# Reordering the last table search, the products of tile 0 and tile 1, and one gather wait in an embedding tower

## The reference

```python
e = jnp.stack([tbl_0[ids[:, 0]], ..., tbl_26[ids[:, 26]]], axis=1)   # 512 x 27 x 128
dot_products = jnp.einsum('bnd,bmd->bnm', e, e)
r, c = np.tril_indices(27, k=-1)
h = jnp.concatenate([dot_products[:, c, r], dense_ctx], axis=1)      # 512 x 367
h = jnp.maximum(h @ W_top1 + b_top1, 0.0)                            # 512
h = jnp.maximum(h @ W_top2 + b_top2, 0.0)                            # 256
y = h @ W_top3
```

## Time and profile before

| what | value |
|---|---|
| median of 3 runs | 108.38 us (107.68 to 108.66) |
| the profiled execution's own time | 108.2 us |
| its span, first to last instruction | 106.3 us |
| TensorE busy, share of the span | 91% |
| VectorE, ScalarE, GpSimd busy | 64% each |
| granted TensorE clock | 1.00 throughout |

### The profile page before, as it was taken

The page is one execution under the profiler, slowest core; times in us unless marked ns, Lnnn a source line. Parts: engine busy times, 40 slices in busy tenths (PEclk is TensorE's granted clock), DMA queues, the critical chain, the costliest instruction groups (busy, mean ns, idle before and its releaser), DMA issues.

```text
span 106.3 us, 3471 instructions
## 1 busy us (share of the span) xinstructions
PE 97.1 (91%) x1496; PEld 78.6 (74%) x1496; DVE 68.5 (64%) x97; ACT 67.6 (64%) x112; POOL 67.7 (64%) x71
## 2 busy tenths in 40 slices
PE   6999879989999998999999989959949999989992
PEld 6646567857788675878788878649849898878981
DVE  5699999999999999999999714016012612007101
ACT  4486999998999969999876008125304555344241
POOL 3777887887778778877877777777777772000000
PEclk9999999999999999999999999999999999999999
DMA  2899749678688773948112222222212211000000
GB/s 49 244 257 199 217 88 294 188 197 240 150 228 272 194 217 70 266 101 227 51 49 56 54 57 52 72 57 56 54 51 56 56 49 49 6 0 6 6 0 1
DMA packets 5305, 12.06 MB, mean 113 GB/s; under 512 B 1765, under 2 KB 2277, under 8 KB 5290
## 3 DMA queue, kind: packets, MB, share of 16 engines
q1 hardware_dynamic: 3282, 7.75, 26.0%
q0 software_dynamic: 1984, 4.07, 15.1%
q10 hardware_dynamic: 24, 0.02, 0.1%
HBM read 11.83 MB, written 0.00 MB: 111 GB/s over the span
## 4 chain that ended last, share of the span: by engine, by line
PE 55%; DVE 34%; issue 7%; ACT 2%; POOL 0%; DVEq 0%; ACTq 0%; POOLq 0%
DVE marks L644 23%; PE gram_ps L537 12%; PE ring L510 11%; DVE low L621 9%; PE ring L590 5%; PE ids_ps L572 4%; PE gram_ps L510 4%; PE ring L521 3%; PE ids_ps L565 3%; PE ring L470 2%; PE ring L600 2%; PE ring L572 2%; PE ids_ps L590 2%; DVE gram L663 1%; PE ring L565 1%
## 5 line engine op out<-in xcount | busy, mean ns | idle before, releaser
L422 POOL DMA_INDIRECT rows<-tbl,ids_sb x62 | 66.7, 1075 | 19.8 <-issue 16.5
L644 DVE TENSOR_TENSOR marks<-ids_ps,row_no 125x1024 fp32r<-125x1024 f32 (+2 forms) x39 | 43.5, 1151 | 0.0
L510 PE MATMUL ring<-marks,high 125*128 125x512 f32 (+1 forms) x64 | 25.5, 399 | 1.3 <-DVE low L621 1.2
L510 PE MATMUL ring<-marks,low 125*128 125x512 f32 (+1 forms) x64 | 24.0, 376 | 0.0
L510 PEld LDWEIGHTS ring<-marks,high 125*128 125x128 f32 x64 | 12.0, 188 | 6.3 <-DVE low L621 3.9
L621 DVE TENSOR_TENSOR low<-raw,high 125x512 fp32r<-125x512 f32 (+1 forms) x23 | 16.3, 708 | 0.0
L537 PE MATMUL gram_ps<-rowsT 128*27 128x27 f32 x1024 | 12.7, 193 | 2.8 <-issue 2.2
L715 ACT ACTIVATE away<-ids_ps,row_no 125x512 f32<-125x512 f32 (+1 forms) x22 | 13.5, 671 | 2.1 <-PE ids_ps L464 2.1
L537 PEld LDWEIGHTS gram_ps<-rowsT 128*27 128x27 f32 x1024 | 10.7, 104 | 5.3 <-issue 3.8
L510 PE MATMUL gram_ps<-marks,high 125*128 125x512 f32 x32 | 13.2, 414 | 0.4 <-DVE low L621 0.4
L701 ACT CAST high<-raw 125x1024 fp32r<-125x1024 f32 (+1 forms) x11 | 12.1, 1097 | 2.2 <-DMA raw<-tbl 2.1
(11 more groups left out here) (61 smaller groups left out, 105.6 us busy)
## 6 DMA issues: line engine op xcount, KB each, us to landing
raw<-tbl SPq DMA_DIRECT2D x9, 448.0 KB
raw<-tbl SPq DMA_DIRECT2D x2, 560.0 KB
rows<-tbl,ids_sb POOLq DMA_INDIRECT x62, 3.0
w_sb<-w SPq DMA_DIRECT2D x2, 256.0 KB
w_sb<-w SPq DMA_DIRECT2D x1, 512.0 KB, 7.9
raw<-tbl SPq DMA_DIRECT2D x9, 52.0 KB
raw<-tbl SPq DMA_DIRECT2D x2, 224.0 KB
w_sb<-w SPq DMA_DIRECT2D x1, 192.0 KB
```

The lines of the kernel that those rows point to most:

```text
L422: nc.gpsimd.indirect_dma_start(out=rows[0:n, i % ROW_BUFS, s, :], out_offset=None, in_=tables[PLACES[s]], in_offset=bass.IndirectOffsetOnA ...
L510: last = nc.tensor.matmul(bank[:, 0:n], part[:, i % SPLIT_BUFS, c * D:(c + 1) * D], mark_of(unit, c), start=c == 0 and part is high, stop= ...
L644: nc.vector.tensor_tensor(marks_of(unit)[:, c0 - c1:, :], index.to_broadcast([TP, c1 - c0, n]), which.to_broadcast([TP, c1 - c0, n]), ALU. ...
```

## The change

Two tables change, and no other line. In `ORDER` both halves of `find 11` now stand ahead of gram 0, where before they stood inside it and behind it; the first two turns of tile 2 stand one in the middle of gram 0 and one behind it; the three pairs of tile 0 stand together in the middle of gram 1; the turns 2 2 and 2 3 come after gram 1, the second one amid l1 of tile 0. In `PACE` gather 48 is held until `products` is 2 (the end of gram 1) instead of `gram_part` 5 (the end of gram 1's second part); the entry of gather 50, which named the same value, goes.

```diff
-find 10 1, gram 0 0, gram 0 1, find 11 0, gram 0 2, gram 0 3, find 11 1, turn 2 0, turn 2 1, gram 1 0
-gram 1 1, gram 1 2, pairs 0 0, pairs 0 1, turn 2 2, pairs 0 2, gram 1 3, turn 2 3, l1 0 0, l1 0 1
+find 10 1, find 11 0, find 11 1, gram 0 0, gram 0 1, turn 2 0, gram 0 2, gram 0 3, turn 2 1, gram 1 0
+gram 1 1, pairs 0 0, pairs 0 1, pairs 0 2, gram 1 2, gram 1 3, turn 2 2, l1 0 0, l1 0 1, turn 2 3
...
-44 gram_part 3, 46 marks_used 50, 48 gram_part 5, 50 products 2, 52 l1_done 1, 54 gram_part 7, 56 paired 6
+44 gram_part 3, 46 marks_used 50, 48 products 2, 52 l1_done 1, 54 gram_part 7, 56 paired 6
```

## The result

The changed kernel takes 111.91 us (median of 6 runs, 110.98 to 114.91) against 108.52 us for the kernel before (6 runs); the ratio is 1.034 (95% interval 1.030 to 1.038). It is 3.4% slower. Some executions of either kernel run a stretch at half clock and are longer for it; the ratios leave them out as far as they stand apart.

What follows compares the result with a forecast made beforehand. TensorE's grams were taken to be bound by their program's arrival in 256-instruction blocks. Three exposed blocks (3.5 + 3.9 + 3.9 us) led to a +3.8 us shift, gathers free: 108.38 + 3.8 = 112.2 us, range 109.4 to 113.4.

Steps and rivals of the forecast that it cites:

- first boundary, in gram 0: End of a 256-instruction program block, 76 matmuls into gram 0, at 63.05 us; expected to cost nothing.
- the three blocks behind it: Next three 256-instruction blocks, through gram 0 and into gram 1, each bound by its transfer: 11.3 us together.
- third boundary behind it: Block end inside gram 1, forecast at 74.35 us where before it was at 70.39: 3.96 us later.
- the block with l1: Block after the stop in gram 1, bound by its own work: 4.86 us before, less 0.1 us.
- shift where gram 2 goes on alike: Delay from gram 2 on, where both orders have the same instructions in the same blocks: +3.85 us.
- The program as the bound: A gram runs at the pace its program arrives; 256 gram instructions want about 1.6 us, get 3.2 to 4.1.
- The cover lost: Find 11's wide matmuls, inside and behind gram 0, partly hid block transfers; moving them ahead of gram 0 exposes these.
- The gathers: Gather 48 held to about 75.25 us, gather 61 landing at 94.0, hidden by 0.3 us; costed at nothing.
- Rival B: Behind gather 48 the last turn waits for a 3.7 us landing: +0.9 us, 113.1 us; chance 0.05.
- Rival A: The program arrives in time in gram 0 and gram 1, so not slower: 107.6 us; chance 0.18.
- Rival C: One more block is stored while TensorE idles at find 11: +2.3 us, 110.7 us; chance 0.07.
- theory C: Arose with the first four runs, not the prediction: stops this close sometimes cost TensorE its clock; no chance given.

## Why the prediction was right

The time came out at 111.91 us where 112.2 was forecast, by the path that the prediction gave. At full clock alone the difference is the forecast's 3.8 us: five executions of the changed kernel have a median of 111.96 us, and 38 of the kernel before, in the later jobs, one of 108.19. The steps, beside what the trace after shows:

| step | forecast | measured |
|---|---|---|
| gram 0 begins | 62.2 us | 62.20 |
| first boundary, in gram 0 | 63.05 us | 63.07, by the count |
| the three blocks behind it | 3.5 + 3.9 + 3.9 = 11.3 us | 3.83 + 3.93 + 3.94 = 11.70 |
| third boundary behind it | 74.35 us | 74.77 |
| the block with l1 | 4.76 us | 4.48 |
| shift where gram 2 goes on alike | +3.85 us | 79.25 - 75.26 = +3.99 |
| gather 48 issued | 75.25 us | 75.79 |
| gather 61 issued | 91.5 us | 92.09 |

*The program as the bound* was right, and it is shown, not only fitted: the stops follow the count of instructions when idle ones are put in, and 256 instructions left out buy a block's passage and not their work. *The cover lost* was right: find 11's move alone makes the loss, and everything else in the change but turn 2 0's new place, put in alone, makes none. *The gathers* were right in size, and their slack was as thin as reckoned: gather 61 landed 2.4 us after its issue, at 94.5 us, and the last turn begins at 94.59. Rival B's late landing did not come.

That single steps agree to some 0.1 us is in part luck, for a block's passage varies between executions. In the second profile of the same kernel the three blocks took 3.28 (from the count's 63.16 us), 3.61 and 3.65 us, 10.5 in all, where this one has 11.70 and the forecast 11.3. In this execution, the slowest of those at full clock, the first block came out 0.33 us over its 3.5, and the block with l1 gave 0.28 us back, so the two errors cancel.

The working also passed over one wait. It let TensorE wait some 1.2 us for VectorE; but with the two finds adjacent, find 11 waits 0.95 us for ScalarE's copy (line 749), which begins only when find 10 has ended. That cost nothing only because VectorE's low part (line 621, 59.87 to 60.55 us) came later still; the first half ended some 0.1 us before the second could begin (60.33 + its 0.17 us of issue, and 60.61). A ScalarE copy 0.2 us longer would have been on the path.

Behind gram 2 the profiled execution lost another 0.5 us (span +4.5 us). One part is the block from 82.58 to 87.00 us, 4.42 us where the earlier trace rows has 4.14. The medians moved by 3.4 (3.8 at full clock), so I don't count it to the change. Rival A is out: the run with 96 idle instructions shows boundaries every 256 that cost 0.98 to 1.60 us each. The Trainium skill ("Runtime: NRT & Kernel Launch", Instruction fetch mechanics) gives TensorE a memory of 2048 instructions and calls such boundaries "mostly hidden"; the measurement decides against it here. Rival C, a block stored up during the finds, is out as well: the first block took 3.83 us, and 3.28 in the second profile, where C gave its own 2.0.

What the prediction did not have is the clock. In some executions TensorE runs at half clock for several us, and the times spread wider than the sizes of the blocks say. The changed kernel lost it in 7 of 12 executions, the kernel before, in the later jobs, in 22 of 60. That the stops cause this, or stops close together (theory C), is not shown.

## What to carry to other kernels

Where an engine shows pauses without a releaser, count its instructions between them, the waits too, before looking for a reason in the code around them; if the count is constant, small instructions are bound by the program's arrival, and their busy time says little. Such a stretch is shortened by fewer instructions (256 fewer bought 3.4 us here). Wide ones put into the same block took a stop away in the runs with l1 amid gram 1, but no time, since other waits came in its place. An edit that gathers small ones together costs the cover even if no wait is added. Price it from the trace's own blocks and give it a range, since the same block took 3.28 us in one execution and 3.83 in another, and test it by moving the boundary with instructions that do nothing.

## What the hardware showed that was not expected

The granted clock of TensorE fell in some executions from full to 0.50, which is 1.2 of its 2.4 GHz, and came back after 3.4 us (74.55 to 77.97 us in the changed kernel's second profile) or 10.2 us (68.91 to 79.15 with the old gather wait). In the six profiled executions that lost it, each fall lies between 0.3 us ahead of the end of a stop and 2.3 us behind it. The run with find 11 put back did so twice in the old order (0.50 from 70.64 and from 80.88 us), behind stops of 1.31 and 1.46 us that stand 9.5 us apart, so it does not take three close together; and the run with 96 idle instructions, which has the most stops, lost it in only 2 of 6 executions. In the run with the old gather wait TensorE had been busy 0.45 of 2.00 us and then 2.03 of 3.90 as the clock fell. In the changed kernel's profiled execution it had been busy even less, and kept its clock:

```profile
64.90:66.90 2.00, 0.17 (x19) 1.00 0.14 35
66.90:70.80 3.90, 2.01 (x128) 1.00 0.21 57
```

So what decides lies not in these two stretches alone. The price is seen in the block with l1: 6.48 and, at full clock, 4.48 us. Whether it falls more often with the earlier gathers was not settled.
